# Attention slots reordered: the transposes of the older pair behind the slot's first product, the exponentials ahead of their copies

## The reference, cut to what matters

```
q = xn @ wq ; k, v = xn @ wkv            # per head 128 wide
scores = q[..., :128] @ k.T * scale       # 4 batches of 256 tokens, 32 heads
scores = where(causal, scores, -1e30)
probs  = softmax(scores)
attn   = probs @ v
x      = x + attn @ wo + expert branch
```

## Time and profile before

| what | value |
|---|---|
| median of 3 runs | 1098.86 us (1098.47 to 1098.95) |
| the profiled execution's own time | 1099.28 us |
| its span, first to last instruction | 1097.4 us |
| PE busy | 1091.9 us (99%) |
| DVE busy | 698.0 us (64%) |
| ACT busy | 542.9 us (49%) |
| POOL busy | 733.7 us (67%) |
| mean granted TensorE clock | 0.999 |
| one round of the MIDDLE loop | 104.5 us (slot 0 at 473.97, next one at 578.50) |

### The profile page before, as it was taken

One profiled execution on the slowest core, in us unless ns is written; L12 is line 12 of the kernel. 1 busy time (PEld: TensorE's weight loads), 2 busy tenths in 40 slices (PEclk: granted clock), 3 DMA queues, 4 the chain that ended last, 5 costly groups with the idle time before them and its releaser, 6 DMA issues.

```text
span 1097.4 us, 21436 instructions
## 1 busy us (share of the span) xinstructions
PE 1091.9 (99%) x6418; PEld 966.2 (88%) x6418; DVE 698.0 (64%) x1761; ACT 542.9 (49%) x1637; POOL 733.7 (67%) x988
## 2 busy tenths in 40 slices
PE   9999999999999999999999999999999999999998
PEld 8887888899998899889988988898899889988987
DVE  7554224376776666766677666766667666776675
ACT  3221132132755665556555645664565566555663
POOL 4656586797955992797299549954994599269910
PEclk9999999999999999999999999999999999999999
DMA  7213331211110120021011101110110012001102
GB/s 240 96 60 104 136 115 49 77 45 32 46 57 3 59 78 21 20 67 49 19 30 66 38 19 58 39 39 19 58 57 22 18 58 77 19 12 59 46 1 77
DMA packets 25287, 59.91 MB, mean 55 GB/s; under 512 B 3585, under 2 KB 3905, under 8 KB 25089
## 3 DMA queue, kind: packets, MB, share of 16 engines
q1 hardware_dynamic: 25216, 59.14, 16.8%
HBM read 57.03 MB, written 2.10 MB: 54 GB/s over the span
## 4 chain that ended last, share of the span: by engine, by line
PE 97%; DMA 1%; POOL 1%; issue 0%; DVE 0%; SPq 0%; ACT 0%; POOLq 0%
PE banks L181 29%; PE banks L182 29%; PE banks L183 29%; PE banks L1719 4%; PE banks L1738 3%; PE banks L1710 3%; DMA gu_stage<-in_w_gu 1%; PE banks L886 0%; PE banks L1015 0%; POOL gu_lo L367 0%; POOL gu_lo L353 0%; PE banks L924 0%; SPq L301 0%; POOL gu_hi L350 0%; PE banks L1001 0%
## 5 line engine op out<-in xcount | busy, mean ns | idle before, releaser
L1285 POOL TENSOR_TENSOR form_lo<-wqk_stage,form_hi 128x256 fp32r<-128x256 f32 x192 | 141.8, 738 | 16.0
L1339 POOL TENSOR_SCALAR vf_hi<-wvo_stage 128x512 fp32r<-128x512 f32 (+1 forms) x48 | 26.3, 548 | 176.6 <-PE banks L183 174.5
L1619 ACT ACTIVATE prob<-prob,top 128x128 f32<-128x128 f32 (+1 forms) x256 | 115.6, 460 | 17.8 <-DVE top L1648 17.6
L1625 ACT ACTIVATE prob<-prob,inv 128x128 f32<-128x128 f32 (+1 forms) x256 | 102.6, 451 | 36.1 <-DVE inv L1654 36.1
L1648 DVE CUSTOM_DVE_ANT_0 prob<-banks,mask 128x128 f32<-128x128 f32 (+1 forms) x256 | 81.3, 355 | 60.3 <-PE banks L183 45.8
L1666 DVE TENSOR_TENSOR acc<-acc,banks 128x512 f32<-128x512 f32 x128 | 86.7, 681 | 36.1 <-PE banks L183 36.0
L181 PE MATMUL banks<-tT_hi,form_hi 128*128 128x512 f32 x256 | 105.6, 412 | 0.0
L182 PE MATMUL banks<-tT_lo,form_hi 128*128 128x512 f32 x256 | 100.2, 391 | 0.0
L183 PE MATMUL banks<-tT_hi,form_lo 128*128 128x512 f32 x256 | 100.1, 391 | 0.0
L181 PE MATMUL banks<-wo_hi,oT_hi 128*128 128x512 f32 x240 | 95.9, 400 | 0.0
L183 PE MATMUL banks<-wo_hi,oT_lo 128*128 128x512 f32 x240 | 93.6, 390 | 0.0
(11 more groups left out here) (309 smaller groups left out, 3590.7 us busy)
## 6 DMA issues: line engine op xcount, KB each, us to landing
wqk_stage<-in_w_qk SPq DMA_DIRECT2D x32, 512.0 KB, 3.3
gu_stage<-in_w_gu SPq DMA_DIRECT2D x21, 512.0 KB, 3.3
wvo_stage<-in_w_v SPq DMA_DIRECT2D x34, 256.0 KB, 2.6
wvo_stage<-in_w_o SPq DMA_DIRECT2D x32, 256.0 KB, 2.7
wd_stage<-in_w_down SPq DMA_DIRECT2D x22, 256.0 KB, 2.6
acc<-in_x SPq DMA_DIRECT2D x8, 256.0 KB, 4.6
out<-acc SPq DMA_DIRECT2D x8, 256.0 KB, 2.0
tab<-in_w_comb SPq DMA_DIRECT2D x1, 1300.0 KB, 6.2
```

Source lines behind the costliest of these rows:

```text
L1285: nc.gpsimd.tensor_tensor(form_lo[:, part], src[:, :], as_f32(form_hi[:, part]), ALU.subtract).then_inc(form_ready, 1)
L1619: ins = nc.scalar.activation(pr, pr, ACT.Exp, bias=top[:, n % 2, r:r + 1], scale=-1.0, accum_out=total[:, n % 2, r:r + 1])
L1625: ins = nc.scalar.activation(pr, pr, ACT.Copy, scale=inv[:, n % 2, r:r + 1])
```

## The change

The helper that puts a pair's steps around a slot's fill is changed; nothing else is.

```diff
     for p, fill in enumerate(slots):
         older = [] if first and p == 0 else [p - 1]
         late = [p - 2] if p % 2 and not (first and p == 1) else []
-        steps += [("S", p)] + [("E", n) for n in late] + [("T", n) for n in older] + [("X", p)]
-        steps += fill[:1] + [("R", p)] + fill[1:]
+        ahead = 1 + [step[0] in "PQW" for step in fill].index(True)
+        steps += [("S", p)] + [("E", n) for n in late] + [("X", p)] + fill[:ahead] + [("T", n) for n in older]
+        steps += [("R", p)] + fill[ahead:]
         steps += [("O", n) for n in older]
```

## The result

The changed kernel takes 1131.38 us (median of 4 runs, 1129.06 to 1132.51), the kernel before 1098.68 beside it: a ratio of 1.0294, 95% interval 1.0278 to 1.031. The forecast was 1133.8. The profiled execution is the fastest of the four, 1129.06, with a span of 1127.3: 29.9 us more than before, where the sum said 34.9. Lines of the new kernel are one higher than before.

What follows compares the result with a forecast made beforehand. PE was taken to bound the kernel, so only new waits count: MIDDLE rounds 18.7, slot 0 4.4, FIRST 5.5, LAST 6.3, together 34.9 us. Median forecast 1133.8 us, range 1122 to 1143, or 1117 to 1148 with neighbours half taken in.

Steps and rivals of the forecast that it cites:

- PE bounds, and only new waits can move it: Whole kernel: PE busy 1091.9 of 1097.4 us, no matmul added or removed, so the change can only make PE wait.
- X ahead of T's copies gains 0: ACT: X starts when DVE has done S, just when the copies are over, so it gets no earlier; gain 0.
- The copies behind the evacuation cost the time: ACT: T's copies wait for the first product's evacuation, so O waits for `pT_lo`, 25 to 28 us over about 31 times.
- Two products, P2 or P3 first: Slots of two products starting with P2 or P3: O at 4.66, loss 1.00, or 1.11 in slot 14 with refill.
- P5 first: Slots starting with P5, two combinations: O loses 1.22 with three products, 2.4 with two; 1.33 in slot 3 with refill.
- Refill: PE after each stall: the next matmul comes late too, 0.11 added per stall, between 0 and 0.11.
- R late, nothing lost: DVE and ACT: R comes 0.7 to 1.3 later, but the next slot's T moved back by 1.4, so nothing is lost.
- Slot 11, 13, LAST's slot 9: Slot 11's P4 waits for its bank, 0.50; slot 13's O late, 0.18; P3 in LAST's slot 9 waits for a bank, 1.05.
- Slot 0: Slot 0 of a loop round: O late and DVE's late last additions delay the loop's turn, 0.89 five times, 4.4 us.
- T behind a product costs PE nothing: PE queue: T takes the same 0.24 behind the first product; bounded by 0.01 us a slot either way, taken as 0.
- The clock: Rival: each of 19 stalls of about 1 us or more lowers PE's clock, 57 us in all, 1190 us; chance 0.03.

Runs made afterwards that it cites:

- copies early on ACT: Changed kernel, but on ACT alone T's copies stand ahead of the first product's evacuation; PE and DVE as changed: 1104.01 us, ratio 1.0048 to the kernel before.
- copies late with PE old: Kernel before on PE (T ahead of the first product), with the changed order on ACT and DVE: 1135.99 us, ratio 1.0339.
- copies early on DVE: Changed kernel with T's copies ahead of the evacuation on ACT, and `pT_lo` ahead of the combinations on DVE where P5 is first: 1104.29 us, ratio 1.0046.
- bare first products: Kernel before with the changed order only in slots whose first product is W, P6 or P7, where nothing is evacuated ahead of T's copies: 1101.00 us, ratio 1.0018.
- slot 0 old: Changed kernel with slot 0 of every group after the first in the order of before: 1130.70 us, ratio 1.0288.

## Why the prediction was right, step by step

- *PE bounds, and only new waits can move it.* Right: the earlier trace rows against the waits after.
- *X ahead of T's copies gains 0.* Right for X. Wrong if read as free: put in alone it costs 27 us, because it makes the copies late.
- *The copies behind the evacuation cost the time.* Shown from both sides: copies early on ACT, 27 of 33 us back; copies late with PE old, all of it lost. The sign came smaller than said, though: waits of O of 18.2 us, 19 times, where I had 25 to 28 over about 31. The other twelve were, by my terms, slot 0 (five) and slot 13 (seven); the first came out as no wait, the second as 0.13 a slot, too short for the list of waits.
- *Two products, P2 or P3 first.* 1.11 expected, 0.94 measured in slot 14. The combination started at 2.16 where I had 2.26, and the evacuation ended at 3.55 where I had 3.64. FIRST's slot 4 gave 0.88 for 1.05, LAST's slot 12 0.94 for 1.11.
- *P5 first.* 1.33 expected, 1.43 measured (slot 3 of MIDDLE), 1.3 and 1.17 in LAST; FIRST 2.54 and 2.48; LAST's slot 11 2.63 and 2.54. The 2.4 for two products does not follow from the text: 1.22 and one product of 1.36 make 2.58, and with the refill 2.69. That the 2.63 came nearer to 2.54 is luck.
- *Refill.* 0.11 expected, 0.12 measured: O's second matmul comes 0.23 after the first instead of 0.11.
- *R late, nothing lost.* Right in the changed kernel: no T waits, but for the final one, 0.08 late where I had 0.25. The run with the copies early on DVE shows the limit; there R is late enough.
- *Slot 11, 13, LAST's slot 9.* 0.50, 0.18 and 1.05 expected; 0.41, 0.13 and 0.92 measured. (FIRST's slots 11, 13 and 14 make 1.79 by these terms, not 1.7.)
- *Slot 0.* The term that failed most, "its last additions end 0.5 later, and if the loop's turn hangs on them so does all this": 0.89 five times, 4.4 us, measured 0.05 to 0.13. The additions did end later, DVE's S came earlier relative to the slot, and O was ready 0.24 to 0.07 ahead. The lateness of S is not counted from the last addition. The 2.75 that I took for that is only DVE's idle time in one round: in the kernel before, the additions end 0.33 to 0.35 after the start of slot 0 in the five late rounds, and S comes 2.92 to 3.77 after it. What the lateness is counted from is open.
- *T behind a product costs PE nothing.* Wrong by 0.03 to 0.05 in slots where a product of 512 columns stands on both sides of T, outside my bound of 0.01: 0.37 in a MIDDLE round of the run with the copies early on ACT (104.91 against 104.54), 2.2 us in six rounds. The run with bare first products shows it in slots without any wait.
- *The clock.* I gave it 57 us and 0.03, as a rival that either comes with every stall of 1 us or not at all. It comes with the stalls of about 2.5 us and not every time, 1.5 to 1.7 us each; without them one run of X ahead alone shows 0.998. The falls are what lies between the profiled run and the median (1129.06 and 1131.38). The Trainium skill's rule (TensorE: Matmul & The Clock Gate, section "HAM oscillation") that idle gaps bring the clock down holds here (granted 0.57 of full in the 4 us behind a stall of 2.3 us), where I had no row for it.

Slot 0 (4.4) and the smaller stalls were put too high by some 7 us together; the spacing left out 2 to 3, and the clock another 2 in the median. The errors cancel: that 1133.8 came as near to 1131.38 as it did is luck. The main terms, slots 3 and 14, and the path through ACT were right by their own measure.

## What to carry to other kernels

Where one list orders several engines, follow a moved step on each engine's own queue. PE could nearly spare the place (0.4 us a round); ACT's copies landed behind an evacuation that waits for DVE. For each chain that ends in the bounding engine, write down when its input is ready and when it is wanted; 1.56 us of slack in a slot of 4.24 was the number that decided. A copy that is ready early belongs ahead of one that still has to wait, and a subtract that frees a bank ahead of work that nobody waits for: that exchange, with T moved in two slots of FIRST, gave 0.12%.

## What the runs showed of the hardware

- One idle time of PE of 2.2 to 2.3 us (the slot is 2.5 longer) was enough for a fall of the granted clock to the lower level, in some executions and not in others. Five kernels have two such idle times; 17 of their 20 runs had a mean clock of 0.998 or 0.997, three had 1.0. A fall cost 1.6 us (slots 11 and 12, same order with and without it), and 512-column matmuls were 0.43 apart. The other seven kernels of the experiments have no idle time above 1.1 us in the attention. Of their 48 runs one had 0.998 (X ahead alone, longest idle time 1.1 us) and one 0.999, the rest 1.0.
- Behind T, whose matmuls are fp32, PE spaces the 512-column fp32r matmuls of the next products wider: in the MIDDLE rounds of the kernel before, the second to seventh are 0.230 to 0.235 apart on average, the eighth to twelfth 0.227. With T between two products the first product has mostly come down to 0.227, and the wide spacing begins anew behind T. That this is the whole of the 0.03 to 0.05 a slot fits, but no run tested it apart. It is still seen in W of slot 1, the second product behind T, which took 1.38 (600.40 to 601.78) instead of 1.36 (589.12 to 590.48):

```profile
600.40 0.39 PE L182 MATMUL banks<-wo_hi,oT_hi 128*128 128x512 f32 x1
...
601.78 0.28 PE L182 MATMUL banks<-pT_hi,v_hi 128*128 128x256 f32 x1
```
```profile
589.12 0.39 PE L181 MATMUL banks<-wo_hi,oT_hi 128*128 128x512 f32 x1
...
590.48 0.28 PE L181 MATMUL banks<-pT_hi,v_hi 128*128 128x256 f32 x1
```

- In the five rounds that follow a jump back of the loop, DVE is idle at the start of slot 0 for nothing the profile shows: 2.6 to 3.4 us in the kernel before, 1.95 to 2.1 in the changed one. The first round and LAST have none of it (S 0.93 and 0.94 after the slot's start). With its last additions over at 0.33 to 0.35, S came 2.92 to 3.77 after the slot's start; with them over at 0.79 to 0.82, in the changed kernel and the one with slot 0 old, 2.74 to 2.92. So the idle time shrinks when the work before it ends later. Over the profiles of all thirteen kernels S came 2.72 to 4.25 after the start of these rounds.
